# Four copies of the batch code against a loop over the first three batches on every engine

## The reference, cut to what matters

```python
mod = (_silu(c) @ wmod).reshape(B, 6, 1, -1)            # sa, ca, ga, sb, cb, gb; gates at least 0.25 in size
h = _layernorm(x) * (1 + ca) + sa
x = x + ga * attn(h)                                    # linear attention: FAVOR+ features, 16 heads of 16
h = _layernorm(x) * (1 + cb) + sb
x = x + gb * ffn(h)                                     # layernorm; q, k, v from 256, 128, 64 or 32 columns
...                                                     # by quarter of the tokens; softmax attention, 8 heads
```

## Time and profile before

| | |
|---|---|
| time, median of 3 runs (lowest, highest) | 2098.27 us (2094.97, 2098.48) |
| the profiled execution: time, span | 2094.97 us, 2093.2 us |
| mean granted clock of TensorE, share of full speed | 0.945 |
| busy share of the span: PE, PEld, DVE, ACT, POOL | 86%, 49%, 72%, 52%, 47% |
| chain that ended last: PE, DVE, ACT, issue, DMA, SPq, POOL | 61%, 21%, 8%, 6%, 2%, 2%, 1% |

### The profile page before, as it was taken

The page is one execution under the profiler, slowest core; times in us unless marked ns, Lnnn a source line. Parts: engine busy times, 40 slices in busy tenths (PEclk is TensorE's granted clock), DMA queues, the critical chain, the costliest instruction groups (busy, mean ns, idle before and its releaser), DMA issues.

```text
span 2093.2 us, 31654 instructions
## 1 busy us (share of the span) xinstructions
PE 1801.3 (86%) x10752; PEld 1035.2 (49%) x10752; DVE 1514.5 (72%) x2733; ACT 1084.0 (52%) x1998; POOL 992.7 (47%) x654
## 2 busy tenths in 40 slices
PE   5788778999888886999988877699998887779997
PEld 3566443444366543444456644344436664434443
DVE  4687677777578677777668857777767876777774
ACT  0566233666566522566646743256665662325664
POOL 0333345666633235566743323656673332356666
PEclk8899988999999997999999999799999998879999
DMA  4000044001200015201020002500111000340011
GB/s 120 1 0 1 1 136 113 16 9 39 61 21 0 1 37 160 54 16 46 4 78 0 0 1 83 163 13 16 39 40 43 0 1 1 127 122 13 12 39 41
DMA packets 55684, 87.12 MB, mean 42 GB/s; under 512 B 13188, under 2 KB 32004, under 8 KB 52868
## 3 DMA queue, kind: packets, MB, share of 16 engines
q1 hardware_dynamic: 55560, 85.54, 14.2%
HBM read 49.68 MB, written 35.70 MB: 41 GB/s over the span
## 4 chain that ended last, share of the span: by engine, by line
PE 61%; DVE 21%; ACT 8%; issue 6%; DMA 2%; SPq 2%; POOL 1%; DVEq 0%; POOLq 0%; ACTq 0%
PE PS L1139 11%; PE PS L1264 10%; PE PS L1252 9%; PE PS L1277 5%; PE PS L1073 4%; PE PS L1041 4%; DVE MXP L827 4%; DVE XSQ L786 4%; PE PS L1065 3%; ACT XSQ L581 3%; PE PS L1182 3%; PE PS L1045 3%; PE PS L1209 2%; DVE QKS L877 2%; ACT QKT L539 1%
## 5 line engine op out<-in xcount | busy, mean ns | idle before, releaser
L827 DVE TENSOR_REDUCE MXP<-PS 128x1 f32<-128x512 f32 x960 | 598.3, 681 | 204.1 <-PE PS L1139 200.6
L486 POOL TENSOR_TENSOR TS<-PR 128x1024 f32<-128x1024 f32 (+1 forms) x256 | 573.2, 2239 | 337.0 <-ACT PR L652 333.4
L652 ACT ACTIVATE PR<-PS 128x512 f32<-128x512 f32 x960 | 504.7, 601 | 427.8 <-PE PS L1252 424.5
L1139 PE MATMUL PS<-KOP,QOP 96*128 96x512 f32 x960 | 422.6, 460 | 46.3 <-DMA KOP<-k_scr 35.5
L1252 PE MATMUL PS<-QOP,KOP 97*128 97x512 f32 x960 | 379.5, 409 | 18.8 <-ACT PR L652 12.7
L1139 PEld LDWEIGHTS PS<-KOP,QOP 96*128 96x128 f32 x960 | 190.7, 200 | 301.9 <-DVE MXP L827 177.6
L1264 PE MATMUL PS<-PR,V 128*32 128x512 f32 x1920 | 273.8, 606 | 0.0
L1073 PE MATMUL PS<-PB,QKT 128*128 128x512 f32 x768 | 221.0, 424 | 31.4 <-DVE QKT L766 31.4
L1252 PEld LDWEIGHTS PS<-QOP,KOP 97*128 97x128 f32 x960 | 181.0, 192 | 86.3 <-ACT PR L652 50.2
L443 POOL TENSOR_SCALAR PK<-XSK 128x1024 f32<-128x1024 f32 x64 | 67.2, 1050 | 284.7 <-ACT XSK L567 242.4
L1073 PEld LDWEIGHTS PS<-PB,QKT 128*128 128x128 f32 x768 | 140.9, 190 | 74.7 <-DVE QKT L766 31.5
(11 more groups left out here) (143 smaller groups left out, 2573.7 us busy)
## 6 DMA issues: line engine op xcount, KB each, us to landing
KOP<-k_scr SPq DMA_DIRECT2D x84, 256.0 KB, 6.1
k_scr<-QKS SPq DMA_DIRECT2D x64, 256.0 KB, 2.8
QOP<-q_scr SPq DMA_DIRECT2D x180, 64.0 KB, 2.0
q_scr<-QKS SPq DMA_DIRECT2D x40, 256.0 KB, 2.8
X<-in_L_attn_x_dram SPq DMA_DIRECT2D x16, 512.0 KB, 4.6
out_dram<-X SPq DMA_DIRECT2D x16, 512.0 KB, 3.1
QOP<-MXT SPq DMA_DIRECT2D x240, 0.5 KB
KOP<-k_scr SPq DMA_DIRECT2D x48, 64.0 KB, 2.0
```

Of the source, the lines that this page charges most:

```text
L486: g.tensor_tensor(sums(k)[:, 0:len(stage)], pair[:, :, 0], pair[:, :, 1], ALU.add).then_inc(S["psum_t"], 1)
L652: a.activation(PR[:, k % 2, w, q], bank(score_bank(p, n, w, q)), ACT.Exp).then_inc(S["ex"], 1)
L827: v.tensor_reduce(MXP[:, u % 2, i, kc:kc + 1], bank(max_bank(p)), AX.X, ALU.max).then_inc(S["am_rd"], 1)
L1139: mm(bank(max_bank(p)), QOP[0:96, u % QS6, i * P:(i + 1) * P], KOP[0:96, h % KS6, kc * CH:(kc + 1) * CH], start=True, stop=True).then_inc( ...
```

## The change

On each of the five engines the first three batches become a loop on the chip over b = 0 to 2, and the last batch is written out behind it. So the program holds two copies of the batch's instructions and no longer four, and in the first of them b is a register: each wait's value that has a term in b, and each address with b in it, is worked out by register instructions while the kernel runs. Inside the tile stage the loop over pairs of tiles is now a loop in a loop. On ACT and POOL `prelude(b + 1)` moves to the end of the loop's body, which leaves the order of work as it was. `PER_B = 202` is the number of increments of DVE's own semaphore in a batch, by which `Chain` works out its counts.

```diff
-    PER_C, PER_P = 12, 9
+    PER_B, PER_C, PER_P = 202, 12, 9
...
-            for b in range(B):
-                batch(b, b == B - 1)
+            with sp.Fori(0, B - 1) as b:
+                batch(b, False)
+            batch(B - 1, True)
...
-            for b in range(B):
-                prelude(b)
+            prelude(0)
+            with pool.Fori(0, B - 1) as b:
                 batch(b)
+                prelude(b + 1)
+            batch(B - 1)
...
-            for b in range(B):
-                prelude(b)
+            prelude(0)
+            with act.Fori(0, B - 1) as b:
                 batch(b)
+                prelude(b + 1)
+            batch(B - 1)
...
-            for b in range(B):
+            with dve.Fori(0, B - 1) as b:
+                own.enter(b, PER_B)
                 batch(b)
-                tail(b, b + 1 if b < B - 1 else None)
+                tail(b, b + 1)
+                own.leave(B - 1)
+            batch(B - 1)
+            tail(B - 1, None)
...
-            for b in range(B):
-                batch(b, b + 1 if b < B - 1 else None)
+            with pe.Fori(0, B - 1) as b:
+                batch(b, b + 1)
+            batch(B - 1, None)
```

## The result

The changed kernel takes 2115.61 us (median of 6 runs, 2107.24 to 2118.84) against 2097.06 us (6 runs, 2094.97 to 2098.48): ratio 1.008, 95% interval 1.0058 to 1.0101. It is slower by 18.5 us. Its profiled execution took 2110.09 us and lies in the lower part of its own range.

What follows compares the result with a forecast made beforehand. It took the order of the stages, and within them mostly PE, as the bound. Six parts summed to 6.0 us a batch, 18 us for three, on 2094.97 us or the median: 2114 us, range 2100 to 2134.

Steps and rivals of the forecast that it cites:

- Parts 1 and 2: Tiles: six written out with register waits cost 0.9 us a batch, ten inner-loop ones with two counters 0.7 us.
- the 0.15: Tiles: a looped tile takes 9.18 us against 9.03 written out, 0.15 us longer, its share of the jump included.
- Part 3: Middle, a 120 us chain like the tiles: register waits lengthen it by the same 1.7%, 2.0 us a batch.
- Part 4: Softmax attention: register waits show only where DVE finishes a unit in slots it holds up, 0.6 us a batch.
- Part 5: Jump back: PE waits 2.75 us for fetched code, 1.25 us are covered, 1.5 us show a batch, three times.
- Part 6: Passage to the next batch: register waits add 1.7% of 18 us, 0.3 us a batch.
- A: Softmax attention loses its pace: each slot 0.07 us longer, about 2126 us, or 2220 with a slow sequencer; chance 0.14.
- D: Softmax attention gets faster: single waits let ACT start 0.06 us earlier a slot, 2083 to 2090 us; chance 0.06.
- B: Inner loops lose their fetched code too: their taken jumps must fetch, 33 us more, 2147 us; chance 0.07.
- C: All of it is covered: looped tile's 0.15 us is its jump, fetch under 1.25 us; 2098 us, no change; chance 0.17.

Runs made afterwards that it cites:

- experiment 4: The kernel before with all 16 tiles of each batch written out and no inner loop: 2092.56 us, ratio 0.9978.
- experiment 7: The changed kernel with a prefetch hint for the outer loop's jump and all 16 tiles written out: 2104.71 us, ratio 1.0035 to the kernel before.
- experiment 5: The changed kernel with PE's block as before, so that only ACT, DVE, POOL and SP loop over batches: 2101.55 us, ratio 1.0017 to the kernel before.
- experiment 2: The changed kernel with a prefetch hint ahead of the outer loop's jump back on all five engines: 2106.34 us, ratio 1.0043 to the kernel before.
- experiment 1: The kernel before with its first two batches in loops of one pass, so b is a register without a jump back: 2102.43 us, ratio 1.0025.
- experiments 1 and 6: Experiment 1, and the kernel before with b a register only in the middle of the first two batches, on all engines: 2102.10 us, ratio 1.0025.
- experiment 3: The changed kernel with only PE looping over batches, the other four engines as before: 2108.39 us, ratio 1.0049 to the kernel before.

## Why the prediction came out as it did

It said 2114 (2100 to 2134) and slower with 0.77; measured were 2115.6 and 2113.05. Point by point:

- **Parts 1 and 2, tiles: too dear, from the right mechanism.** Predicted 1.6 us a batch; the tile stages of the three looped batches became longer by 1.0 us in all. Tiles 1 to 11 of the second batch, where a second counter enters the value, take 692.70 - 601.12 = 91.58 us against 91.53: nothing, the lower bound. Written-out tiles with register waits, 12 to 15, take 33.36 us against 33.01 (12 and 13 alone: 710.93 - 692.70 = 18.23 against 703.97 - 685.92 = 18.05), 0.09 a tile and not 0.15. So the step that was mis-sized is the 0.15. The 0.15 came from one distance; ten looped tiles give 0.10 (experiment 4). Where the 0.09 arises, one hand-over shows. Timeline of the kernel after, second batch, ACT's second exponential of tiles 1, 11, 12 and 13 and PE's weight load behind that of tile 12; and PE's instructions on the line of the two waits ahead of this load (L1070), around 702.9:

```profile
601.12 1.06 ACT L584 ACTIVATE XSQ<-XSQ 128x1024 f32<-128x1024 f32 x1 [0.56 <-DVE XSQ L791]
...
692.70 1.06 ACT L584 ACTIVATE XSQ<-XSQ 128x1024 f32<-128x1024 f32 x1 [0.57 <-DVE XSQ L791]
701.81 1.06 ACT L584 ACTIVATE XSQ<-XSQ 128x1024 f32<-128x1024 f32 x1 [0.57 <-DVE XSQ L791]
...
703.00 0.42 PEld L1074 LDWEIGHTS PS<-ident,XSQ 128*128 128x128 f32 x4 [1.07 <-issue]
...
710.93 1.06 ACT L584 ACTIVATE XSQ<-XSQ 128x1024 f32<-128x1024 f32 x1 [0.57 <-DVE XSQ L791]
```

```profile
L1070 PEldq ALU_OP  x1: 36/36/36, 702.9 to 702.9; - x1
```

The same in experiment 7, which has register waits and no inner loop (tile 12, and the line of the two waits over the whole tile stage):

```profile
696.61 1.06 ACT L576 ACTIVATE XSQ<-XSQ 128x1024 f32<-128x1024 f32 x1 [0.56 <-DVE XSQ L783]
...
697.72 0.42 PEld L1066 LDWEIGHTS PS<-ident,XSQ 128*128 128x128 f32 x4 [0.99 <-ACT XSQ L576]
```

```profile
L1062 PEldq EVENT_SEMAPHORE  x14: 51/51/51, 604.8 to 720.6; - x14
L1062 PEldq ALU_OP  x1: 36/36/36, 597.9 to 597.9; - x1
```

In the first, ACT ends at 702.87, then PE works out the second wait's value (702.9) and goes on at 703.00, 0.13 later. In the second PE goes on 0.05 after ACT, although b is a register there too: the line is a plain wait in 14 tiles and an ALU_OP in one only, and tiles 12 to 15 take 33.13 us. This is the prediction's mechanism, a value worked out behind the first of two waits, and it also shows that a register wait costs it only where the arithmetic is left at that place. Why the same source lines came out in one order here and in another there is open.

- **Part 3, middle: right in size, half right in cause.** Predicted 2.0 us, measured 2.06 on average over all traces (2.8 a batch in the ledger). But waits are 0.9 of it (0.7 at the higher clock), and the rest goes with the lower clock, which the prediction did not have. At which hand-overs the 0.9 us arise was not read. That the sum of the two met the estimate is chance.
- **Part 4, softmax attention: too dear.** Predicted 0.6 us a batch, measured -0.3 over all four. Where PE's rate is the bound, the register work is hidden whole.
- **Part 5, the jump: too cheap, and counted once too often.** Predicted 2.75 us of waiting less 1.25 us of cover, 1.5 us, three times. Measured: 3.84 us of idle PE less the 0.84 that were there before, 3.0 us, and 3.4 and 3.2 us in the passages, twice: 6.6 against 4.5. The term that was mis-sized is the wait: the jump took 3.98 and 3.79 us, not 2.75. The cover was about right: PE begins its jump at 576.61, while the transposes of 576.50 still run, and without a stall it would have gone on at 577.76, so 1.15 us were free. That the jumps of DVE and ACT are covered held in this kernel, where PE is later than they are; where PE does not jump, DVE's shows by 0.5 and 0.2 us (experiment 5), since its code takes 3.0 to 3.4 us and not 2.6. That the hint removes the stall shows its kind (experiment 2). The jumps over a batch waited, while no inner loop's jump in the kernel after took PE more than 0.25 us. The rule of the Trainium skill that the prediction cites, "Runtime: NRT & Kernel Launch", section "Instruction fetch mechanics", that a taken branch to code outside the held window has to wait for a fetch, agrees with this. That each engine would stall at each of three jumps held for four engines at two jumps; on SP the next instruction came after 0.3 us.
- **Part 6, register waits in the passage: nothing.** 21.99 and 21.96 us in experiment 1 against 22.81 and 22.48, which is within what such passages scatter.
- **The sum.** 18 us predicted. Measured 18.5 and 15.4 us by the two comparisons, 14.7 in the ledger. Parts 1, 2, 4 and 6 were too high by some 7 us in all, part 5 too low by 2; the middle drew 8.2 us in this execution where the forecast has 6.0 and the average over the traces is 6.2. That the sum came so near is luck: its terms are off by more than the sum is, and they cancel. The medians vary with the clock by more than this: the changed kernel's own executions go from 2107.24 to 2118.84 us.

The rivals: A and D needed slots of another length, and the softmax attention kept its length to 0.7 us of 223 in every batch. B needed stalls in inner loops; ten looped tiles take what they took. C had the jump covered and the waits at nothing: it was right of most waits, wrong of the jump and the middle.

**Open:** whether and why register waits lengthen the low stretches of the clock. In experiments 1 and 6 the late one came with registers in the middle and without any jump, in experiment 3 with PE's registers alone; with those of the others alone (experiment 5) it did not come in three middles. Whether slightly longer stops of PE tip the grant, or only the moment at which the middle begins, no run tested. Open too are the fourth hinted jump, and whether experiment 2 gained more than its passages: 2.7 us by one median, 0.1 by the other.

## What to carry to other kernels

Rolling a long body into a loop costs by the stage: nothing where an engine's own rate is the bound, a little at each hand-over at which a wait's value is worked out behind another wait, and at each jump back the wait for code that isn't there any more, less what the engine would have idled anyway; look up which engine's idle time at the jump is shortest (and which is next, for when the first is mended), count the jumps that are taken (passes less one), and try a hint on the jump first. Where a stage sits between the clock's two levels, compare many of its instances sorted by the granted clock before a microsecond is put down to an edit: here a difference of 1.6 us came without any edit. And when a price is read from a looped and an unlooped copy, one distance between events is a thin base; the sum over ten tiles was a third lower.

## What the runs showed of the hardware that was not expected

- A jump back over a whole batch's code took PE 3.7 to 4.5 us in seven cases over four traces (3.6 to 4.35 us of idle time), where one packet on its queue takes about 1 us by the earlier trace rows. The first instruction behind the jump came after 3.0 to 3.4 us on DVE, 4.6 to 4.8 on ACT and 3.3 to 4.3 on POOL, but after 0.3 on SP, whose body is the shortest (257 instructions a batch; POOL's has 530, PE's 3490). With a hint ahead of it, PE's jump cost nothing at three of four.
- Of two waits in a row with register values, the second one's arithmetic stands behind the first wait or not, as the code comes out: the hand-over takes 0.13 us or 0.05.
- An inner loop of two tiles costs 0.10 us for each tile of 9.1 us: written out, the kernel before becomes 4.7 us faster (0.9978), though the queues then bring 86 + 65 packets of code and no longer 69 + 55.
- The same instructions in the same stage took 121.0 or 122.6 us, as the clock at its start was granted (PEclk of the first 14 us 0.77 to 0.88, or 0.63), and changed from batch to batch within one execution.
